# Local attention of layer L2 cut into finer pieces, with a new order of pieces from the seam behind the mamba layer on

## The reference

```python
x = x + _layernorm(_L0_attn_ref(_layernorm(x), ...))   # Mamba and top-2 of 8 experts
x = x + _layernorm(_L0_ffn_ref(_layernorm(x), ...))    # top-8 of 64 experts and 2 shared
x = x + _layernorm(_L1_attn_ref(_layernorm(x), ...))   # WKV recurrence
x = x + _layernorm(_L1_ffn_ref(_layernorm(x), ...))    # ternary linear layer
x = x + _layernorm(_L2_attn_ref(_layernorm(x), ...))   # local attention
x = x + _layernorm(_L2_ffn_ref(_layernorm(x), ...))    # one of 8 linear maps by position
x = x + _layernorm(_L3_attn_ref(_layernorm(x), ...))   # Lorentz attention
x = x + _layernorm(_L3_ffn_ref(_layernorm(x), ...))    # top-2 of 8 experts and a shared one
```

```python
q = rope(q)
k = rope(k)
attn = jnp.einsum('bhqd,bhkd->bhqk', q, k) * scale
mask = (j <= i) & (j > i - WIN)
attn = jnp.where(mask[None, None], attn, -jnp.inf)
attn = jax.nn.softmax(attn, axis=-1)
out = jnp.einsum('bhqk,bhkd->bhqd', attn, v)
return out.transpose(0, 2, 1, 3).reshape(B, T, H * HD) @ Wout
```

## Time and profile before

| | us |
|---|---|
| runs | 1418.59, 1418.81, 1420.58 (median 1418.81) |
| profiled execution, its own time | 1419.12 |
| its span, first to last instruction | 1417.3 |
| PE busy | 1098.8 (78%) |
| VectorE busy | 975.5 (69%) |
| ScalarE busy | 714.4 (50%) |
| GpSimd busy | 614.4 (43%) |
| mean granted clock of TensorE | 0.887 |

### The profile page before, as it was taken

The page is one execution under the profiler, slowest core; times in us unless marked ns, Lnnn a source line. Parts: engine busy times, 40 slices in busy tenths (PEclk is TensorE's granted clock), DMA queues, the critical chain, the costliest instruction groups (busy, mean ns, idle before and its releaser), DMA issues.

```text
span 1417.3 us, 13196 instructions
## 1 busy us (share of the span) xinstructions
PE 1098.8 (78%) x3858; PEld 574.3 (41%) x3858; DVE 975.5 (69%) x2190; ACT 714.4 (50%) x1368; POOL 614.4 (43%) x426
## 2 busy tenths in 40 slices
...
DMA packets 11271, 17.76 MB, mean 13 GB/s; under 512 B 1304, under 2 KB 7584, under 8 KB 10688
## 3 DMA queue, kind: packets, MB, share of 16 engines
...
## 4 chain that ended last, share of the span: by engine, by line
PE 38%; DVE 11%; ACT 7%; POOL 3%; issue 3%; POOLq 0%; DVEq 0%; ACTq 0%
PE bankE L1833 6%; PE bankE L1218 3%; ACT b_pr L1116 2%; PE bankS L1796 2%; PE bankE L1750 2%; PE bankE L1280 2%; PE bankS L1750 2%; PE bankS L1781 2%; PE bankS L1753 1%; PE bankE L1239 1%; PE bankE L615 1%; PE bankE L1753 1%; PE bankS L1723 1%; PE bankE L575 1%; PE bankE L608 1%
## 5 line engine op out<-in xcount | busy, mean ns | idle before, releaser
L727 DVE TENSOR_TENSOR_SCAN hs<-dA,carry,bankS 128x512 f32<-128x512 f32 x128 | 156.7, 1265 | 3.2
L331 POOL TENSOR_TENSOR hc<-hs,cb 128x1024 f32<-128x1024 f32 x56 | 131.9, 2356 | 35.1 <-DVE hs L727 32.3
L306 POOL TENSOR_TENSOR cv<-cv,hc 128x1024 f32<-128x1024 f32 x56 | 132.1, 2358 | 4.4
L1708 ACT ACTIVATE c_h<-bankE,C 128x512 f32<-128x512 f32 x144 | 98.7, 687 | 52.4 <-PE bankE L1833 50.1
L1602 POOL TENSOR_TENSOR c_acc<-c_acc,c_tw 128x512 f32<-128x512 f32 x32 | 46.0, 1436 | 159.1 <-DVE c_tw L1927 159.0
L439 ACT ACTIVATE sg<-bankE,C 128x512 f32<-128x512 f32 x80 | 54.9, 687 | 82.5 <-PE bankE L575 82.4
L719 DVE TENSOR_TENSOR bankS<-dx,bankS 128x1024 f32<-128x1024 f32 x64 | 78.3, 1223 | 6.7 <-PE bankS L504 6.1
L1833 PE MATMUL bankE<-c_fH,c_w1H 128*128 128x512 f32 x144 | 80.9, 562 | 1.1 <-ACT c_h L1708 1.1
L392 ACT ACTIVATE dA<-dl,Aneg 128x512 f32<-128x512 f32 x128 | 80.2, 708 | 0.1
L615 PE MATMUL bankE<-hh,f 128*128 128x512 f32 x128 | 70.4, 631 | 10.3 <-DVE hh L837 10.3
L538 PE MATMUL bankE<-h2T,wg 128*128 128x512 f32 x128 | 72.1, 646 | 3.5 <-ACT sg L420 1.4
...
## 6 DMA issues: line engine op xcount, KB each, us to landing
...
```

Source lines behind the costliest of these rows:

```text
L306: pool.tensor_tensor(cv[:, :, :], cv[:, :, :], (hv if by_vector(i, k) else hc)[:, :, :], ALU.add).then_inc(s["y_acc"], 1)
L331: pool.tensor_tensor(dst[:, :, :], hs[:, k % HS, :, :], cb[:, k % 2, :].unsqueeze(1).to_broadcast([P, HV, G]), ALU.mult).then_inc(s["hc_re ...
L727: V.tensor_tensor_scan(hs[:, k % HS, h, :], dA[:, (HV * k + q) % DA, :], dbx[:, h, :], carry[:, k, h:h + 1], ALU.mult, ALU.add).then_inc(s ...
L1708: act.activation(h[:, n % 3, :], E[k % 2][:, :], ACT.Gelu_apprx_tanh, bias=col("b1_3", k)).then_inc(s["fs_ready"], 1)
```

## The change

The pieces are cut finer. ScalarE's piece c is 5 exponentials (two banks) and a new piece d the 3 others. V is V (four heads) and v (four more). ScalarE's copy of the value products is a piece w of its own, and its copy of the projection a piece o; PE's W and O are as they were. PE's V waits also for `b_oaT` of the tile before.

The list is the same up to `aB2.3` (422 of the 1025 old entries); behind it the order is new, 1089 entries in all. In the tiles the old order was C(k+1) V(k) H(k) c(k+1) W(k) O(k) C(k+2); the new one is C(k+1) V(k) c(k+1) d(k+1) v(k) H(k) C(k+2) W(k) w(k) c(k+2) d(k+2) O(k). Other pieces move too, of which the diff shows the main ones. Names in brackets are the piece that the entry now stands behind; the list has no brackets.

```diff
-    ... aU18.2 aU19.2 aL2.2 aB2.3 bP0.0
-    aL6.2 aL7.2 aR1.3 bP1.0 bP2.0 aR3.3 bP3.0 aR4.3 bP4.0 aM0.3 bP5.0 bK1.0 ...
+    ... aU18.2 aU19.2 aL2.2 aB2.3 bP0.0 aR1.3 bP1.0 aR3.3 bP2.0
+    aR4.3 aL6.2 bP3.0 bP4.0 aL7.2 aM0.3 bP5.0 bK1.0 ...
...
-    aL4.3 aL5.3 bK3.1 aR2.3 aU0.3 aR5.3 bK13.1 aR6.3 aU1.3 aU2.3 bK4.1 ...
+    aL4.3 aL5.3 bK3.1 aR2.3 aU0.3 aR5.3 bK13.1 bK4.1 aR6.3 bK14.1 aU1.3 ...
...
-    ... bA10.0 bK3.2 bQ0.0 bQ1.0 bQ2.0 bQ3.0 bC0.0 bK13.2 bc0.0 bN0.0 bA0.1 bC1.0 bV0.0 bH0.0
-    bc1.0 bK4.2 bN1.0 bK14.2 cS0.0 bW0.0 bO0.0 bC2.0 bK5.2 bV1.0 bK8.2 cS1.0 bH1.0 bc2.0 bW1.0 bO1.0 bN2.0 cS2.0 bK15.2 bC3.0 bV2.0 bH2.0
-    bc3.0 bK16.2 bW2.0 bK7.2 bN3.0 bK9.2 bK6.2 bO2.0 bK10.2 bV3.0 bH3.0 bW3.0 cS3.0 bA10.1 bO3.0 bK17.2 bK1.3 bA1.0 cS4.0 bQ0.1 cS5.0 cS6.0
-    bK11.3 bA11.0 bQ1.1 bA12.0 bQ2.1 bA3.0 bX0.0 bK2.3 bK3.3 bK13.3 bX1.0 ... bX7.0 bA4.0 bQ3.1 bA2.0 bC0.1 ...
+    ... bA10.0 bK3.2 bQ0.0 bQ1.0 cS0.0 bQ2.0 cS1.0 bQ3.0 bC0.0 bK13.2 bc0.0 cS2.0 bd0.0 cS3.0 bN0.0 bA0.1 bC1.0 bK4.2
+    bV0.0 bc1.0 bd1.0 bv0.0 bH0.0 bN1.0 bC2.0 bc2.0 bW0.0 bw0.0 bd2.0 bK14.2 bN2.0 bK5.2 bK8.2 bK15.2 bO0.0 bo0.0 bV1.0 bv1.0 bH1.0 bW1.0
+    bC3.0 cS4.0 bw1.0 bO1.0 bo1.0 bV2.0 bv2.0 bH2.0 bW2.0 bc3.0 bd3.0 bK16.2 bw2.0 bK7.2 bO2.0 cS5.0 bo2.0 bN3.0 bK9.2 bK6.2 bV3.0 bK10.2
+    bv3.0 bH3.0 bW3.0 bw3.0 bA10.1 bO3.0 bo3.0 bK17.2 bK1.3 bQ0.1 cS6.0 bA1.0 bQ1.1 bQ2.1 bA11.0 bQ3.1 bK11.3 bA12.0 bA3.0 bX0.0 ...
+    bX5.0 bK2.3 bX6.0 bX7.0 bA4.0 bK3.3 bA2.0 bC0.1 ...
...
-    bQ2.2 bK7.3 bK9.3 bK6.3 bA11.1 bQ3.2 bA12.1 bK10.3 bK17.3 bA3.1 bX0.1 ...
+    bK7.3 bK9.3 bK6.3 bK10.3 bA12.1 bQ2.2 bA3.1 bK17.3 bQ3.2 bX0.1 ...
...
-    bN0.2 cI0.0 bA0.3 cQ0.0 bC1.2
-    bV0.2 bH0.2 bc1.2 bN1.2 bW0.2 bO0.2 bC2.2 bV1.2 bH1.2 bc2.2 bW1.2 bO1.2 bN2.2 bC3.2 bV2.2 bH2.2 bc3.2 cG0.0 cQ1.0 bW2.2 bN3.2 bO2.2
-    bV3.2 bH3.2 bA10.3 bW3.2 cG1.0 bO3.2 ...
+    bA13.1 bN0.2 bA0.3 bC1.2 bV0.2 bc1.2 bd1.2 bv0.2 bN1.2 bH0.2 bC2.2 bW0.2 bw0.2 bc2.2 bd2.2 bO0.2 bo0.2 cI0.0 cQ0.0 bV1.2 bv1.2
+    bH1.2 bN2.2 bC3.2 bc3.2 bW1.2 bw1.2 bd3.2 bO1.2 bo1.2 bV2.2 bv2.2 bH2.2 cG0.0 cQ1.0 bW2.2 bw2.2 bO2.2 bo2.2 bN3.2 bV3.2 bv3.2 bH3.2
+    bA10.3 bW3.2 bw3.2 cG1.0 bO3.2 bo3.2 ...
...
-    cR2.0 cR3.0 cU0.0 cy1.0 cU1.0 ... cs0.0 [behind cZ6.1] ... cs1.0 [U19.1] ... cs2.0 [U29.1] cs3.0 [U34.1] cs4.0 [O0.1]
-    cO1.1 cs5.0 cs6.0 cU4.2 ... cU16.2 cR0.3 cs7.0 ... cU21.2 cs8.0 cR1.3 ... cU33.2 cR3.3 cU34.2
+    cR2.0 cI1.0 cy1.0 cU0.0 cW1.0 cR3.0 ... cs0.0 [behind t3.1] cs1.0 [Y0.1] ... cs2.0 [U12.1] cs3.0 [X0.1] ... cs4.0 [t7.1] ... cs5.0 [U26.1]
+    ... cs6.0 cs7.0 [X1.1] ... cO0.1 cR3.2 ... cU6.2 cs8.0 ... cU20.2 cR1.3 cU21.2 ... cO0.2 cR3.3 cU2.3
...
-            elif p[0] == "c":
+            elif p[0] in "cd":
...
-                for h in HEADS[2] + HEADS[0] + HEADS[1]:
+                for h in HEADS[2] + HEADS[0] if p[0] == "c" else HEADS[1]:
...
-            elif p[0] == "V":
-                for w in range(2):
-                    at_least(act, s["b_pTp"], e, 3 * T, 3 * k + w + 1)
-                    act.activation(pT[:, 4 * w:4 * w + 4, :], F[(k + w) % 2]..., ACT.Copy).then_inc(s["b_pT"], 1)
+            elif p[0] in "Vv":
+                w = int(p[0] == "v")
+                at_least(act, s["b_pTp"], e, 3 * T, 3 * k + w + 1)
+                act.activation(pT[:, 4 * w:4 * w + 4, :], F[(k + w) % 2]..., ACT.Copy).then_inc(s["b_pT"], 1)
...
-            elif p[0] == "W":
+            elif p[0] == "w":
                 at_least(act, s["b_ot"], e, T, k + 1)
...
-            elif p[0] == "O":
+            elif p[0] == "o":
                 at_least(act, s["b_yo"], e, T, k + 1)
...
-            elif p[0] == "V":
-                A, B = F[k % 2], F[1 - k % 2]
+            elif p[0] in "Vv":
+                w = int(p[0] == "v")
                 at_least(pe, s["b_pn"], e, T, k + 1)
-                for w, bank in enumerate((A, B)):
-                    if w == 1 and k > 0:
-                        at_least(pe, s["b_yc"], e, T, k)
-                    for h in range(4): ...
-                    mm.then_inc(s["b_pTp"], 1)
+                if w == 0 and k > 0:
+                    at_least(pe, s["b_oaT"], e, T, k)
+                if w == 1 and k > 0:
+                    at_least(pe, s["b_yc"], e, T, k)
+                for h in range(4): ...
+                mm.then_inc(s["b_pTp"], 1)
```

More of the change, by code:

```diff
@@ L101 @@
[L101 to L112, removed]
@@ L133 @@
[L133 to L136, removed]
@@ L145 @@
-    cO0.3 cO1.3 cO2.3
-""".split()]
+    aF1.0 aF5.0 aF6.0 aF2.0 aF0.0 aF7.0 aF3.0 aF8.0 aF9.0 aA0.0 aN0.0 an0.0 ao0.0 aN1.0 an1.0 aA1.0 aA2.0 ao1.0 aN2.0 an2.0 ao2.0 aN3.0
+    an3.0 ao3.0 aN4.0 aA3.0 an4.0 ao4.0 aN5.0 aA4.0 an5.0 aA5.0 ao5.0 aN6.0 aA6.0 an6.0 ao6.0 aN7.0 an7.0 ao7.0 aN8.0 an8.0 ao8.0 aN9.0
+    aA7.0 an9.0 ao9.0 aN10.0 an10.0 ao10.0 aN11.0 an11.0 ao11.0 aN12.0 an12.0 ao12.0 aN13.0 an13.0 ao13.0 aN14.0 an14.0 ao14.0 aN15.0 an15.0
+    ao15.0 aB1.0 aB3.0 aB4.0 aB2.0 aF1.1 aF5.1 aM0.0 aF6.1 aF2.1 aF0.1 aF7.1 aM1.0 aF3.1 aF8.1 aR1.0 aF9.1 aA0.1 aR3.0 aA1.1 aR4.0 aN0.1
@@ new lines @@
+    bK2.2 aL7.3 bD0.0 bA0.0 bA10.0 bK3.2 bQ0.0 bQ1.0 cS0.0 bQ2.0 cS1.0 bQ3.0 bC0.0 bK13.2 bc0.0 cS2.0 bd0.0 cS3.0 bN0.0 bA0.1 bC1.0 bK4.2
+    bV0.0 bc1.0 bd1.0 bv0.0 bH0.0 bN1.0 bC2.0 bc2.0 bW0.0 bw0.0 bd2.0 bK14.2 bN2.0 bK5.2 bK8.2 bK15.2 bO0.0 bo0.0 bV1.0 bv1.0 bH1.0 bW1.0
+    bC3.0 cS4.0 bw1.0 bO1.0 bo1.0 bV2.0 bv2.0 bH2.0 bW2.0 bc3.0 bd3.0 bK16.2 bw2.0 bK7.2 bO2.0 cS5.0 bo2.0 bN3.0 bK9.2 bK6.2 bV3.0 bK10.2
+    bv3.0 bH3.0 bW3.0 bw3.0 bA10.1 bO3.0 bo3.0 bK17.2 bK1.3 bQ0.1 cS6.0 bA1.0 bQ1.1 bQ2.1 bA11.0 bQ3.1 bK11.3 bA12.0 bA3.0 bX0.0 bX1.0 bX2.0
@@ new lines @@
+    bd0.3 bA13.2 bN0.3 cZ4.0 cY0.0 bC1.3 bV0.3 bv0.3 bH0.3 bW0.3 bc1.3 bd1.3 cy0.0 bN1.3 bC2.3 bw0.3 bO0.3 bo0.3 bV1.3 bv1.3 bH1.3 cW0.0
+    bc2.3 bd2.3 bN2.3 cZ5.0 cE4.0 cV0.0 bW1.3 bw1.3 bC3.3 bO1.3 bo1.3 bV2.3 bv2.3 bH2.3 bc3.3 bd3.3 bN3.3 bW2.3 bw2.3 cZ6.0 bO2.3 bo2.3
+    bV3.3 bv3.3 bH3.3 cT4.0 bW3.3 bw3.3 ct4.0 bO3.3 bo3.3 bA1.3 cZ7.0 cE5.0 bA11.3 bA12.3 bA3.3 cX0.0 cT5.0 ct5.0 bX0.3 cE6.0 cT6.0 bX1.3
+    bX2.3 bX3.3 bX4.3 bX5.3 bX6.3 bX7.3 ct6.0 cE7.0 bA4.3 cT7.0 bA2.3 ct7.0 cY1.0 bA13.3 cR0.0 cR1.0 cR2.0 cI1.0 cy1.0 cU0.0 cW1.0 cR3.0
@@ new lines @@
+    cV1.0 cX1.0 cQ0.1 cU1.0 cU2.0 cU3.0 cU4.0 cU5.0 cU6.0 cU7.0 cG0.1 cU8.0 cQ1.1 cG1.1 cU9.0 cU10.0 cU11.0 cU12.0 cU13.0 cH0.1 cZ0.1 cU14.0
+    cU15.0 cU16.0 cU17.0 cU18.0 cR0.1 cU19.0 cU20.0 cR1.1 cU21.0 cU22.0 cU23.0 cU24.0 cU25.0 cR2.1 cZ1.1 cE0.1 cU26.0 cU27.0 cZ2.1 cE1.1
+    cT0.1 cU28.0 cU29.0 ct0.1 cZ3.1 cT1.1 cU30.0 cU31.0 cU32.0 cU33.0 ct1.1 cE2.1 cE3.1 cS8.0 cU34.0 cR3.1 cZ4.1 cT2.1 cU35.0 cU0.1 cU1.1
+    cO0.0 cU2.1 cU3.1 cO1.0 cU4.1 ct2.1 cE4.1 cU5.1 cT3.1 cU6.1 ct3.1 cs0.0 cZ5.1 cE5.1 cY0.1 cs1.0 cO2.0 cU7.1 cy0.1 cZ6.1 cW0.1 cU8.1
```

70 lines of the change are left out of this document (38 added, 32 removed).

## The result

The changed kernel took 1429.57 us (median of 4 runs, 1425.70 to 1430.97), the kernel before 1419.69 (4 runs, 1418.59 to 1421.96). The ratio is 1.0058, 95% interval 1.0044 to 1.0072: slower by 0.6%, where 0.4% faster was forecast. The profiled execution of the changed kernel took 1430.97 us. Ratios are of fast executions: one of e11_last_part_warm, 5212 us, is left out.

What follows compares the result with a forecast made beforehand. Outside stretches where PE is full, chains of waits bound the kernel, in attention a ring through three engines. Terms 3.7 - 4.0 + 1.9 - 2.6 + 0.4 - 1.7 - 3.0 = -5.3 us gave 1413.5 us, range 1404 to 1425.

Steps and rivals of the forecast that it cites:

- The code: Split loops and extra wait instructions in the attention pieces: same work, costed at nothing.
- Attention tiles: Four attention groups: +2.4, +0.3, +1.1 and -0.1 us for groups 0 to 3, together +3.7.
- the ring: Chain of waits through three engines per attention tile: 8.71 us to shrink to 7.7, 2.9 less in a group.
- the drain: Work left behind tile 3's exponentials in an attention group: 4.0 us longer, from W2, O2 and a copy.
- The rival of the clock: Attention tiles: PE's idle time lowers its clock, some 4 us a group, +16 in all, 1429.5 us; chance 0.06.
- The rival of the drain in full: Attention groups: ring doesn't shrink, each pays 4.0 us, 16 instead of 3.7, total 1425.8 us; chance 0.14.
- Way to group 1: From attention group 0 to 1: Q1 and Q2 come before two norms, -4.0 us, bounds 0 and -6.7.
- Way to group 2: From attention group 1 to 2: X's products go behind Q3, +1.9 us, bounds 0 and +3.
- Way to group 3: From attention group 2 to 3: the prediction gave it no term.
- The seam: Behind the mamba layer: b_wcol's wait of 4.5 us shrinks, M0.3 starts 3.4 earlier; -2.6 with K4.1's +0.8.
- Start of the last layer: Start of the last expert layer: PE fills its 3.2 us wait for c_wt with U0's products, -1.7 us.
- The end: Last expert layer: 4.82 us norm wait nearly goes (-4.5), one stretched cast costs +1.5; together -3.0 us.

Runs made afterwards that it cites:

- e11_last_part_warm: Old list with the new order from U0.1 on, plus six unused products behind tile 0's scores in all four groups, against the kernel before: 1.0018.
- e1: The finer pieces and the new wait in V with the old list order, against the kernel before: 1.0000.
- e9: New tile order in group 2 alone, with ScalarE's copies w0 and w1 put behind d2 and d3, against the kernel before: 1.0043.
- e10: New tile order in group 2 alone, plus six unused products on PE behind the scores of tile 0, against the kernel before: 1.0020.
- e3: Old list with the new order only from Q1.0 to U0.1 (attention groups, Lorentz attention, first U pieces), against the kernel before: 1.0049.
- e7: New order in the seam alone, with SP starting the four transfers P1 needs before the WKV weights, against the kernel before: 0.9982.
- e6: Old list with the new order in the seam alone (P1 to M0.3), against the kernel before: 1.0019.
- e16: Old seam, new order from M4.3 to Q1.0 (experts of group 3, WKV pieces of group 1), old list behind, against the kernel before: 0.9979.
- e12: Old list with the new order only from R0.0 of the last experts to U0.1, cS7.0 put in front, against the kernel before: 1.0020.
- e4: Old list with the new order only from U0.1 of the last experts to the end, against the kernel before: 0.9962.

## Why the prediction was wrong

*The code.* Costed at nothing, and that is what e1 measured.

*Attention tiles.* Forecast +3.7, measured in the four groups +2.1, +2.5, +3.6 and -1.6 (9.37 - 7.31 and so on from the traces; the last two are 8.92 - 5.37 and 9.75 - 11.32), +6.5. Group 0 came near (+2.4). In group 2 the term that was mis-sized is the ring's: -2.9 in three tiles were forecast and -1.1 came. What stays behind tile 3's exponentials, the drain, came out at +4.7 for the forecast +4.0, and that is luck: W2 and O2, which made up the sum, stood behind c3 in the old list as well, where they ran under tile 3's exponentials (970.72 to 974.97). What is new behind c3 is O1, V2 and H2, since the new list gives each tile's products a later place, so that V3, which followed N3 by 2.8 us, follows it by 7.1. Two things were left out of the ring: W and ScalarE's w stand between scores and exponentials in the new list, and the clock. e9 shows that moving w alone wins 2.2 at tile 2 and loses more behind it. The rival of the clock named the right thing and had its price wrong: +4 in each group were set, and e10 gives it 0.8 in group 2; the mask takes 1.25, 0.87 and 0.70, the first as of old. The rival of the drain in full held in group 2 for the greater part, and not in the sum. Group 1 was not taken apart.

*Way to group 1.* Forecast -4.0, measured -5.1 in the changed kernel and -5.2 in e3: right in sign, and within the bounds. *Way to group 2*: +1.9 forecast, -1.4 came: the sign was wrong. *Way to group 3*: nothing forecast, +2.4 came, in e3 too. Pieces of lane c and X pieces changed places there; that this is the cause was not shown.

*The seam.* This is the step that failed: -2.6 with K4.1, measured +7.4 at Q0.0. The prediction took the wait of 4.5 us for b_wcol as one on VectorE's row alone, of which 3.4 would go, and did not ask what came next. It was a transfer that comes only 0.9 us before the old time (e7). M0.3's products came 1.2 us later instead of 3.4 earlier, since P3's copies stand behind R4.3 and L6.2 now, and by 632 us it was 3.6, most of it at the lower clock. The seam makes 3.4 of the loss (e6). The new order of WKV pieces and experts behind it, of which only K4.1 was costed (+0.8), gives 4.2 alone (e16); where in that stretch it arises was not taken apart, so this half of the step's cause stays open.

*Start of the last layer.* Forecast -1.7: the wait for c_wt did shrink, by 1.2, but Lorentz pieces moved in the same list make PE wait elsewhere (2.2 us for c_pT), which was costed at nothing, and c_wt of the next group comes 4.0 later (e12).

*The end.* Forecast -3.0, measured -6.6 in e4 and -4.9 in the changed kernel. The mechanism was half right: the norm of R1.3 comes earlier, but the casts are still stretched, by another operation of GpSimd, so its wait is 2.5 us and not near nothing. What makes the win is that wait (2.35 shorter), about 1.1 on R1.3's transposes and routing products, which are no longer at the lower clock throughout (1.12 to 0.66, 1.87 to 1.26 in e4), 1.1 for a wait ahead of them that is gone, and about 1.7 before and behind, where PE's waits for c_acc shrank from 3.8 to 2.2; the forecast had only the first. The next products run at 0.62 to 0.78 instead of 0.40 in all three kernels: 6 of them in the kernel before and in e4, 13 in the changed kernel, which is a part of what that one lacks against e4.

The sum from the trace, 7.4 - 0.1 + 6.5 - 4.1 + 4.5 - 4.9 = 9.3, is the 9.4 of the profile. Seam and WKV part together are 10 us off the forecast, the attention 2.8, the start of the last layer 6.2.
